# Who issues the keys' cluster weights: GpSimd instead of SyncE, in the opening of a two-block transformer kernel

## The reference

```
q, k, v = x Wq, x Wk, x Wv                       # 16 heads, 8 features each
qb = softmax(q Whq); kb = softmax(k Whk)         # 32 cluster weights for each token and head
logits = q k / sqrt(8) + 0.1 * (qb kb)
attn = softmax(logits);  out = (attn v) Wo
```

## Time and profile before

| what | value |
|---|---|
| median of 3 runs | 3410.33 us (3407.64 to 3416.72) |
| profiled execution, its own time | 3410.16 us |
| its span | 3408.2 us |
| PE, DVE, ACT, POOL busy, of the whole span | 93%, 75%, 50%, 59% |
| q1, the hardware queue that SP issues to | 160144 packets, 33.0% of 16 engines |
| queue of transfers issued by POOL | none in the trace |

### The profile page before, as it was taken

The page is one execution under the profiler, slowest core; times in us unless marked ns, Lnnn a source line. Parts: engine busy times, 40 slices in busy tenths (PEclk is TensorE's granted clock), DMA queues, the critical chain, the costliest instruction groups (busy, mean ns, idle before and its releaser), DMA issues. The chain is left out here.

```text
span 3408.2 us, 51407 instructions
## 1 busy us (share of the span) xinstructions
PE 3177.4 (93%) x17792; PEld 2098.5 (62%) x17792; DVE 2570.4 (75%) x3764; ACT 1699.8 (50%) x3077; POOL 2019.1 (59%) x1573
## 2 busy tenths in 40 slices
PE   5899998599999999999999999999999999999998
PEld 3455554466666577666665776666657766666576
DVE  7788775478788677787886778878867778788666
ACT  4566666433443465534434655344346553443465
POOL 2000000367877765778777657787776576877765
PEclk8899998699999999999999999999999999999999
DMA  5433410422232155322321553223216532232153
GB/s 120 73 69 60 81 44 13 109 68 63 66 75 60 26 183 146 89 60 66 75 60 26 183 145 89 60 66 75 60 26 183 145 87 62 66 75 60 26 175 112
DMA packets 160401, 283.60 MB, mean 83 GB/s; under 512 B 32592, under 2 KB 64208, under 8 KB 159888
## 3 DMA queue, kind: packets, MB, share of 16 engines
q1 hardware_dynamic: 160144, 280.31, 33.0%
HBM read 88.47 MB, written 31.72 MB: 35 GB/s over the span
## 5 line engine op out<-in xcount | busy, mean ns | idle before, releaser
L1304 ACT ACTIVATE prob<-psA 128x512 f32<-128x512 f32 x1152 | 652.3, 595 | 1048.4 <-PE psA L1651 454.1
L1134 POOL TENSOR_TENSOR xw<-xw,prob 128x512 f32<-128x512 f32 x672 | 872.0, 1298 | 228.8 <-ACT prob L1304 154.3
L1960 DVE TENSOR_REDUCE mxp<-psA 128x1 f32<-128x512 f32 (+3 forms) x864 | 528.7, 664 | 60.9 <-PE psA L1627 37.6
L1934 DVE RECIPROCAL rden<-psA 128x256 f32<-128x256 f32 x256 | 449.0, 1754 | 135.1 <-PE psA L1682 132.1
L1650 PE MATMUL psA<-qs,ks 128*128 128x512 f32 x1152 | 525.8, 456 | 20.2 <-ACT prob L1304 17.0
L1627 PE MATMUL psA<-ks,qs 128*128 128x512 f32 (+3 forms) x1536 | 476.7, 386 | 13.3 <-DMA qs<-qs 8.7
L1157 POOL TENSOR_TENSOR hidl<-gate,hidh 128x512 fp32r<-128x512 f32 x256 | 331.3, 1302 | 221.4 <-ACT hidh L1354 218.9
L1134 POOL TENSOR_TENSOR xw<-prob 128x512 f32<-128x512 f32 x224 | 293.7, 1311 | 283.2 <-ACT prob L1304 142.4
L1651 PE MATMUL psA<-qs,ks 128*128 128x512 f32 x1152 | 452.1, 392 | 0.0
L1887 DVE TENSOR_REDUCE mxp<-psA 128x1 f32<-128x1024 f32 x256 | 304.7, 1220 | 83.0 <-PE psA L1472 81.8
L1227 ACT ACTIVATE pr<-psA 128x512 f32<-128x512 f32 x512 | 275.6, 600 | 131.8 <-PE psA L1491 123.5
(11 more groups left out here) (213 smaller groups left out, 5833.1 us busy)
## 6 DMA issues: line engine op xcount, KB each, us to landing
qs<-normed SPq DMA_DIRECT2D x256, 256.0 KB, 4.3
rbp<-rab SPq DMA_DIRECT2D x256, 192.0 KB, 3.4
spread<-routing_weights SPq DMA_DIRECT2D x128, 256.0 KB, 3.6
qs<-qs SPq DMA_DIRECT2D x64, 256.0 KB, 3.4
expert_weight_halves<-eh SPq DMA_DIRECT2D x32, 384.0 KB, 2.4
expert_weight_halves<-el SPq DMA_DIRECT2D x32, 384.0 KB, 3.6
eh<-expert_weight_halves SPq DMA_DIRECT2D x32, 384.0 KB, 3.2
el<-expert_weight_halves SPq DMA_DIRECT2D x32, 384.0 KB, 3.9
```

The costliest lines, as they stand in the source:

```text
L1134: g.tensor_tensor(psum_k[:, t % 2, :], before, prob[:, i % 4, :], ALU.add).then_inc(s_su, 1 if kt > 1 else 2 + (t == 1))
L1304: act(prob[:, k % 4, :], psS[:, k % 2, :], ACT.Exp, scale=float(HD) ** -0.5).then_inc(s_ex, 1)
L1934: vec.reciprocal(rden[:, :], psO[t % 2][:, 256:512]).then_inc(s_rd, 1)
L1960: vec.tensor_reduce(dst, bank, AX.X, ALU.max).then_inc(s_mr, 1)
```

## The change

The transfers of the keys' cluster weights (TD and TE with s = 1) are issued by POOL, on its own queue. Those of the queries stay with SP. The plan lists them under their new engine with the costs that they had, so `planned()` runs on another plan and may order every engine's list of the opening anew. The 14 small loads now follow TE(0,0) on SP. The number of transfers and what each moves is as before.

```
+            by = ("sync", "gpsimd")[s]
+            stage(by, ("TD", p, s), 5000, ("scalar", ("TH", p, s)), free)
+            stage(by, ("TE", p, s), 2500, ("vector", ("TL", p, s)), (by, ("TD", p, s)))
+            stage("land", ("TD", p, s), 3500, (by, ("TE", p, s)), ("sync", ("TQ", p, s)))
...
-                    for h in range(HG):
-                        put(s, r, 32 if s else 64, h, tlo[s][h * NB:(h + 1) * NB, :])
-                    if p == 0 and s == 1:
+                        put(r, 64, h, tlo[0][h * NB:(h + 1) * NB, :])
+                    if p == 0:
...
+            def put(r, row, h, src):
+
+                nc.gpsimd.dma_start(kst[r][row:row + NB, h, :].bitcast(F32), src.bitcast(F32)).then_inc(s_td[1], 16)
...
+                elif what == "TD":
+                    p, s = i
+                    r = p % STACKS
+                    if p >= STACKS:
+                        g_.wait_ge(s_qk1, (p - STACKS + 1) * N_S1)
+                    elif p:
+                        g_.wait_ge(s_qd[0], 128)
+                        g_.wait_ge(s_qd[1], 128)
+                    g_.wait_ge(s_th, 2 * p + s + 1)
+                    for h in range(HG):
+                        for row in (0, 64):
+                            put(r, row, h, thi[1][h * NB:(h + 1) * NB, :])
+                elif what == "TE":
+                    p, s = i
+                    g_.wait_ge(s_tl, 2 * p + s + 1)
+                    for h in range(HG):
+                        put(p % STACKS, 32, h, tlo[1][h * NB:(h + 1) * NB, :])
```

More of the change, by code:

```diff
@@ L267, in opening_order @@
             stage("sync", ("TQ", p, s), 3700 - 1800 * s, free, stored)
-            stage("sync", ("TD", p, s), 5000, ("scalar", ("TH", p, s)), free)
-            stage("sync", ("TE", p, s), 2500, ("vector", ("TL", p, s)), ("sync", ("TD", p, s)))
-            stage("land", ("TD", p, s), 3500, ("sync", ("TE", p, s)), ("sync", ("TQ", p, s)))
+            by = ("sync", "gpsimd")[s]
+            stage(by, ("TD", p, s), 5000, ("scalar", ("TH", p, s)), free)
+            stage(by, ("TE", p, s), 2500, ("vector", ("TL", p, s)), (by, ("TD", p, s)))
+            stage("land", ("TD", p, s), 3500, (by, ("TE", p, s)), ("sync", ("TQ", p, s)))
         for c in range(2):
@@ L877, in _ @@
                     sp.dma_start(bd[h * F1:(h + 1) * F1, i, h * NB:(h + 1) * NB], w[h]).then_inc(s_w1, 16)
[L878 to L883, removed]
+            def put(r, row, h, src):
+                sp.dma_start(qst[r][row:row + NB, :, h, :].bitcast(F32), src.bitcast(F32).rearrange("f (c n) -> f c n", c=2)).then_inc(s_td[0], 16)
             for what, *i in OPENING["sync"]:
@@ L902, in _ @@
                     for h in range(HG):
-                        for row in ((0, 64) if s else (0, 32)):
-                            put(s, r, row, h, thi[s][h * NB:(h + 1) * NB, :])
+                        for row in (0, 32):
+                            put(r, row, h, thi[0][h * NB:(h + 1) * NB, :])
                 elif what == "TQ":
```

## The result

The changed kernel takes 3437.39 us (median of 4 runs, 3435.97 to 3442.17). The kernel before took 3411.1 us on the same chip (4 runs, 3407.64 to 3416.72). The ratio is 1.0078, with a 95% interval of 1.006 to 1.0095: slower by 26 us. The forecast was 3405.0 and its range ended at 3433.

What follows compares the result with a forecast made beforehand. The prediction took the opening's steady passes as bound by PE. From 3410.16 us it took off 7.2 gained before the first S and added 2 lost in passes 2 to 7, giving 3405.0 us; range 3399 to 3433.

Steps and rivals of the forecast that it cites:

- What bounds the kernel: In the opening's first 620 us, the steady passes are bound by PE; work hidden below it costs nothing.
- SP is freed of 8.8 us: In pass 0, 12 of 24 puts leave SP, saving 8.8 us; TQ starts 9.0 us earlier, at 66.6.
- 7.2 us gained before the first S: In the start, `mrow` lands at 97.5, so S follows VT at 99.43 instead of 106.67: 7.2 us gained.
- A put costs POOL 1.1 us: On POOL, each put takes 1.1 us, between 0.63 and 1.91; 12 puts of a pass take 13.2 us.
- The rival with 0.26: At the first M of passes 2 to 7, POOL issues slowly, eating the gain at 1.16 us a put; chance 0.26.
- 3 us or more each would be the slow POOL: Sign: PE's waits for `kst` before the first M of passes 2 to 7 would show POOL issuing slowly.
- Pass 0 and pass 1 at no cost: At the first M of passes 0 and 1, no gain or loss; pass 1 is covered by 1.3 us only.
- Landing 3.5 us after the last put; distance 16.3 us; 2 us lost: Passes 2 to 7: keys' puts land 16.8 us after TH, against 16.3 to M; 0.3 a pass, 2 us lost.
- slow POOL at 1.5 us a put: Before the first M of passes 2 to 7, 5.3 us lost a pass, 32 in all: 3435; rival's chance 0.26.
- The costly plan: The new plan places the first M up to 3.5 us sooner behind TH, costing up to 21 us: 3426; chance 0.06.
- The "likeliest" case, no measurable change: Whole kernel: time stays within 0.3% (10.2 us) of the kernel before; chance 0.60.

Runs made afterwards that it cites:

- experiment 1: Against the kernel before: only the issue of the keys' puts moved to POOL, every engine keeping its old order; 3428.43 us, ratio 1.0048.
- Experiment 6: POOL issues the keys' puts in the old order, with TQ of passes 2 to 7 moved behind JR(p-2,1), against the kernel before; 3398.91 us, ratio 0.9966.
- Experiment 9: The kernel before, with only TQ(3,1) to TQ(7,1) put ahead of the keys' puts of the pass before in SP's list; 3449.09 us, ratio 1.0106.
- experiment 3: The changed kernel with only TQ(p+1) moved behind TE(p,0) in SP's list, passes 2 to 6; 3406.89 us, ratio 0.9989 to the kernel before.
- experiment 4: The changed kernel with landing planned at 9000 ns instead of 3500 and M planned to wait for both sides; 3438.9 us, ratio 1.0078.
- experiment 7: The kernel before, SP issuing everything, with TQ of passes 2 to 7 moved behind JR(p-2,1); 3396.7 us, ratio 0.9964.
- experiment 2: The changed kernel's new plan and lists, but with SP issuing all 24 puts of a pass; 3434.56 us, ratio 1.0065 to the kernel before.

## Why the prediction was wrong

- **What bounds the kernel**: right. The passes are bound by PE, the landing of the puts had next to no slack, and all of the loss is in the opening. The network part is 2777.9 us long against 2780.9, within what it varies.
- **SP is freed of 8.8 us**: the puts went, but QD 2 started at 63.95, not 58.8, and TQ at 72.00, not 66.6. The four `qst<-tlo` puts took 4.52 us instead of 2.5, and the small loads behind them 9.6 instead of 7.2, while POOL's puts were in the engines. 3.6 of the 9.0 us came, and TQ left the engines at about 97.5 us, not 90.
- **7.2 us gained before the first S**: not obtained; 1.1. `mrow` did stop mattering. What took its place is the new order of T and VT on PE. The forecast let S follow VT at 99.43 in the old order; the lists were made anew and I did not work them out for the start. Even with the old order (experiment 1) only 3.7 us came, since `mrow` still took 8.4 us to land behind TQ. Experiment 6, which also takes TQ(2) out of the start, has S at 99.87.
- **A put costs POOL 1.1 us**: wrong, 0.49. The rival with 0.26, and the slow side of the range with it, rested on a cost that is less than half of what was taken. Its sign came all the same: "3 us or more each would be the slow POOL" was met by waits of 3.3 to 5.1 us that have another cause.
- **Pass 0 and pass 1 at no cost**: right, to 0.5 us in pass 0 (first M at 64.41 us after a wait of 4.75, before at 64.91 after 2.70). No wait at the first M of pass 1.
- **Landing 3.5 us after the last put; distance 16.3 us; 2 us lost**: this is the step that failed, and in it the landing. Passes 2 to 6 cost 29.1 us where 2 were counted for passes 2 to 7. The distance was right: in pass 3 PE came to M 15.8 us behind the end of TH(3,1). The issue took 5.85 us instead of 13.2. The landing was 11 us instead of 3.5 (medians of `kst<-tlo` and `qst<-tlo`), and in three of the five waits the last to land was the queries', which the sum did not have at all. I took a range of 2.4 to 7.1 from a trace in which SP's order kept TQ's second part behind the keys' puts, and treated TQ only where it hurt before, in the start. Yet that part of the prediction had the row that mattered: share 0.47 for TQ at 64 GB/s. I did not ask where TQ goes once SP's list is shorter. Nor did the sum, or any rival's price, have the clock: a wait was counted at its own length, and the half clock behind the five waits added 12 us. Experiment 9 has the place of TQ alone and costs 38 us; experiment 3 takes it away and the loss is gone.
- **The rivals**: slow POOL at 1.5 us a put gave 3435, nearest to the 3437.4 measured, and that is luck, since a put took 0.49. The costly plan gave 3426 at 6 in 100. The place of both was right (the first M of passes 2 to 6), and a part of the second's reason: the new order does cost when TQ stands where it stood. Its mechanism was not: M was not too early behind TH, the puts were late. With M planned later the time was 3438.9 (experiment 4), and with the new order kept but TQ moved, 3406.9 (experiment 3).
- The "likeliest" case, no measurable change, is refuted; the direction was given 0.28.

What stays open: SP itself is sometimes busy longer with the same puts, four in 4.3 to 5.1 us instead of 2.5 in kernels in which POOL issues too. It is not the second queue alone. In the kernel before SP took 4.11 us for four in pass 3 with no other issuer (at 231.54), and in experiment 7 it took 3.81 for four. What sets it was not tested. Nor was it tested which of the new order's steps costs the 4.6 us in the start.

## What to carry to other kernels

When a list of transfers gets shorter, ask what moves up in it, and whether that is work that nobody waits for yet. A prefetch belongs behind the transfers whose landing is awaited, in the quiet time after them, and all the more so one that uses only half of the engines, since here it held up the transfers behind it by its whole length there (experiment 9). Read DMA share and GB/s together: here a share near 1 at half of the usual rate was such a transfer. A planner that counts landing as a fixed delay cannot see this. Here it helped to correct the place of the transfer, and not to correct the constant. And price a wait of PE with the clock behind it.

## What the runs showed of the hardware

- A put of 32 x 4 KB issued by POOL takes 0.49 us of POOL (12 in 5.85), less than SP's 0.63, and with TQ out of the way it does not matter who issues in passes 2 to 6: 292.8 and 292.9 us from F(2) to F(7) in kernels 6 and 7.
- Transfers of 8 rows from DRAM move 64 GB/s at a DMA share of 0.47, while the puts that are left at a share of 0.53 (the last row of experiment 9) move 135. So for the same busy time in the engines they move about half as much.
- After each wait of 3.3 to 6.3 us before M, in the changed kernel and in experiment 9, PE worked on for 3 to 6 us at a granted clock of 0.50 (1.2 GHz) before it was back at 1.00. In the changed kernel this made 12 us out of 20.5 us of waits, more than half as much again. Shorter waits differed: behind 2.38 us (experiment 1, pass 6) and 2.48 us (experiment 2, pass 3) the clock stayed at 1.00, behind 2.28 us (experiment 2, pass 2) PE worked at 0.50 for about 3.5 us.
